# A two-layer graph network on one core: the turn from the edge sums to layer 1 in another order

## The reference, cut to what matters

```python
h = max(layernorm(x), 0)
agg = segment_sum(edge_attr_64, dst) / max(count, 1)        # per node, width 64
x = x + (relu(concat([agg, h]) @ W1 + b1) @ W2 + b2)         # layer 0, hidden width 512
h = max(layernorm(x), 0)
neigh = segment_sum(h[src], dst) / max(deg, 1)
x = x + (h @ w_self.T + b_self + neigh @ w_neigh.T)          # layer 1
```

## Time and profile before

| | us |
|---|---|
| median of 3 runs | 1263.76 (1263.55 to 1265.26) |
| the profiled execution | 1267.12 |
| its span in the profile | 1265.2 |
| PE busy | 1182.2 |
| DVE busy | 786.3 |
| ACT busy | 517.8 |
| POOL busy | 422.6 |

### The profile page before, as it was taken

The page is one execution under the profiler, slowest core; times in us unless marked ns, Lnnn a source line. Parts: engine busy times, 40 slices in busy tenths (PEclk is TensorE's granted clock), DMA queues, the critical chain, the costliest instruction groups (busy, mean ns, idle before and its releaser), DMA issues.

```text
span 1265.2 us, 31863 instructions
## 1 busy us (share of the span) xinstructions
PE 1182.2 (93%) x11708; PEld 928.3 (73%) x11708; DVE 786.3 (62%) x1710; ACT 517.8 (41%) x982; POOL 422.6 (33%) x384
## 2 busy tenths in 40 slices
PE   2879999999999899779999999999999999999997
PEld 1778888888888788647777767777776776777774
DVE  3537566566666455576666676666666676675762
ACT  3582133233233135344444444444444444444441
POOL 3001010010100166234634545435444453453451
PEclk9878999999999899879999999999999999999999
DMA  3895444444444411111212212112122121121221
GB/s 109 267 313 164 133 115 127 118 124 133 115 125 118 161 57 57 44 47 55 76 55 63 68 55 70 55 54 74 55 63 63 54 75 55 52 77 55 63 63 41
DMA packets 67053, 116.03 MB, mean 92 GB/s; under 512 B 10644, under 2 KB 30824, under 8 KB 66962
## 3 DMA queue, kind: packets, MB, share of 16 engines
q1 hardware_dynamic: 51922, 75.12, 19.5%
q0 software_dynamic: 15040, 39.80, 11.3%
HBM read 101.93 MB, written 12.95 MB: 91 GB/s over the span
## 4 chain that ended last, share of the span: by engine, by line
PE 80%; DVE 5%; DMA 5%; issue 3%; POOL 3%; DVEq 2%; ACT 2%; SPq 0%; ACTq 0%
PE bank L1093 33%; PE couples L888 14%; PE couples L1086 9%; PE bank L1112 7%; PE bank L923 6%; PE bank L913 4%; POOL kreg L570 3%; PE bank L911 3%; PE bank L1104 2%; DMA kreg<-in_edge_attr_dram 1%; DVE oreg L1518 1%; DMA hreg<-in_dst_dram 1%; DMA kreg<-in_src_dram,startu 1%; PE bank L1124 1%; PE couples L880 1%
## 5 line engine op out<-in xcount | busy, mean ns | idle before, releaser
L1093 PE MATMUL bank<-hreg,areg 128*128 128x512 f16 x2058 | 504.9, 382 | 0.0
L588 POOL DMA_INDIRECT wide<-h_table,aggn x280 | 324.6, 1159 | 400.3 <-PE couples L1086 230.4
L770 ACT ACTIVATE areg<-couples 128x784 bf16<-128x784 f32 x336 | 276.4, 823 | 376.7 <-PE couples L1086 375.0
L1093 PEld LDWEIGHTS bank<-hreg,areg 128*128 128x128 bf16 x2058 | 265.7, 144 | 104.6 <-issue 1.3
L888 PEld LDWEIGHTS couples<-oreg,kreg 128*64 128x64 f32 x3232 | 208.7, 145 | 44.4 <-issue 32.1
L888 PE MATMUL couples<-oreg,kreg 128*64 128x48 f32 x3232 | 220.4, 230 | 19.8 <-DMA kreg<-in_edge_attr_dram 11.2
L1518 DVE TENSOR_TENSOR oreg<-iota,kreg 128x1024 bf16<-128x1024 f16 x336 | 195.7, 624 | 51.5 <-PE couples L1086 49.9
L1518 DVE TENSOR_TENSOR hids<-iota,kreg 128x1024 bf16<-128x1024 f16 x336 | 196.3, 625 | 45.0 <-PE couples L1086 44.7
L889 PE MATMUL couples<-oreg,ones 128*64 128x48 bf16 x1616 | 202.0, 213 | 0.0
L889 PEld LDWEIGHTS couples<-oreg,ones 128*64 128x64 bf16 x1616 | 168.3, 109 | 0.0
L555 POOL TENSOR_TENSOR xr<-xr,b2bc 128x512 f32 x25 | 32.5, 1301 | 336.3 <-ACT h0buf L674 336.3
(11 more groups left out here) (165 smaller groups left out, 1048.2 us busy)
## 6 DMA issues: line engine op xcount, KB each, us to landing
kreg<-in_edge_attr_dram SPq DMA_DIRECT2D x202, 256.0 KB, 2.9
h_table<-hreg SPq DMA_DIRECT2D x25, 256.0 KB
xr<-in_x_dram SPq DMA_DIRECT2D x6, 1024.0 KB, 7.9
out_dram<-hbuf SPq DMA_DIRECT2D x42, 128.0 KB
wide<-h_table,aggn POOLq DMA_INDIRECT x280
wide<-in_L_gnn_W_dram SPq DMA_DIRECT2D x2, 512.0 KB, 6.7
out_dram<-h0buf SPq DMA_DIRECT2D x6, 128.0 KB
hreg<-in_dst_dram SPq DMA_DIRECT2D x1, 512.0 KB
```

Of the source, the lines that this page charges most:

```text
L588: pool.indirect_dma_start(near[:, k, :], None, table, bass.IndirectOffsetOnAxis(ap=nearsrc[:, n * GHALF + k:n * GHALF + k + 1], axis=0)).t ...
L770: act.activation(step.rearrange("p (a k) -> p a k", a=2), cpl[s % 2][:, :, 0:BC * KEYS], ACT.Copy).then_inc(s_adj, 1)
L1093: ins = pe.matmul(bank[4 + par], adj[:, par, :, h], htab[:, h, :], start=(h == 0), stop=(h == TN - 1))
```

## The change

On TensorE the 50 count transposes are split: 36 (the tiles of pairs 0 to 8, whose counts are final by then) are issued after the last `outer` of the last span, before the branch; 14 stay behind the wait for the finished `acc`. They go to bank 3 rather than bank 0. In `layer0` of pairs 9 to 11 `outer(i, 0)` stands ahead of the first `key_transposes`. `couples(0, 0)` and `couples(0, 1)` stand ahead of `outer(12, 0)`. On VectorE `low_part` stands ahead of `keys` in pairs 8 to 10; pair 11 has moved in among the first one-hots, and `low_part(12, 0)` behind the eighth. On ScalarE pair 11's two `h1` have moved behind `copy_places(2)` and `hidden(12, 0)`, in among the first copies of counts. TensorE has a wait for the table at step 5 of dense product 1, where ScalarE's wait for the same two semaphores is still ahead of its first copy for the next tile.

```diff
             layer0(BESIDE)                    # ScalarE
-            for n in range(3):
+            for n in range(2):
                 layer0(KEY0 + n, n)
+            hidden(U // 2 - 1, 0)
+            hidden(U // 2 - 1, 1, own=1)
+            copy_keys(2)
+            for q in range(2):
+                sd_of(U // 2 - 1, q)
+            copy_places(2)
             hidden(U // 2, 0)
...
             for s in range(ST):
-                if s == 2:
+                if s < 2:
+                    h1(U // 2 - 1, s)
+                if s == 4:
                     sd_of(U // 2, 0)
                     h1(U // 2, 0)
                 copy_counts(0, 0, s)
...
+                        if j == 16 and size < SPAN * SLOTS:   # TensorE, the last span
+                            complete_counts()
...
             pe.wait_ge(s_acc, 1)
-            for t in range(T):
-                ins = pe.transpose(bank[0][:, t:t + 1], acc[FE:FE + 1, t * P:(t + 1) * P], ident[FE:FE + 1, FE:FE + 1])
-            ins.then_inc(s_cntp, 1)
+            counts_by_node(4 * (BESIDE + 1), T).then_inc(s_cntp, 1)
...
+                outer(i, 0, 0)
+                outer(i, 0, 1)
                 if n is not None:
                     key_transposes(n, key16[n % 2], s_keytr)
-                for q in range(2):
-                    outer(i, q, 0)
-                    outer(i, q, 1)
+                outer(i, 1, 0)
+                outer(i, 1, 1)
...
+            hidden(U // 2, 0, 0, own=1)
+            hidden(U // 2, 0, 1, own=1)
             for s in range(ST):
                 couples(0, s)
                 if s == 1:
+                    outer(U // 2, 0, 0)
+                    outer(U // 2, 0, 1)
                     near_transposes()
...
+                        if first and s == 5:
+                            pe.wait_ge(s_tab[1], U // 2)
+                            pe.wait_ge(s_tab[0], U // 2 + 1)
...
+                low_part(i, 0)                 # VectorE, layer0
+                low_part(i, 1)
                 if n is not None:
                     keys(n)
-                low_part(i, 0)
-                low_part(i, 1)
...
+            last = U // 2
+            mean_by(last, 0)
             dve.wait_ge(s_loT, 1)
-            for s in range(ST):
+            dve.wait_ge(s_keys, NK)
+            one_hots(0, 0)
+            x1_stats(last - 1, 0)
+            x1_stats(last - 1, 1)
+            ln1(last - 1, 0)
+            ln1(last - 1, 1)
+            one_hots(0, 1)
+            near_in()
+            one_hots(0, 2)
+            low_part(last - 1, 0)
+            one_hots(0, 3)
+            x1_stats(last, 0)
+            ln1(last, 0)
+            one_hots(0, 4)
+            low_part(last - 1, 1)
+            near_out()
+            for s in range(5, ST):
                 one_hots(0, s)
-                if s == 1:
-                    near_in()
-                    x1_stats(U // 2, 0)
-                    ln1(U // 2, 0)
-                if s == 3:
-                    low_part(U // 2, 0)
-                    near_out()
+            low_part(last, 0)
```

More of the change, by code:

```diff
@@ L926, in outer, with counts_by_node, complete_counts @@
                     ins.then_inc(s_outp[q], 1)
+            def counts_by_node(t0, t1):
+                for t in range(t0, t1):
+                    ins = pe.transpose(bank[3][:, t:t + 1], acc[FE:FE + 1, t * P:(t + 1) * P], ident[FE:FE + 1, FE:FE + 1])
+                return ins
+            def complete_counts():
+                pe.wait_ge(s_h0T, U)
+                for q in range(2):
+                    pe.wait_ge(s_agg[q], BESIDE + 1)
+                counts_by_node(0, 4 * (BESIDE + 1))
             parts = {0: (hidden, 0, 0), 2: (hidden, 0, 1), 4: (hidden, 1, 0), 7: (hidden, 1, 1),
@@ L1054, in _ @@
                 layer0(KEY0 + n, n)
[L1055 to L1058, removed]
             def near_transposes():
@@ L1363, in mean_by, with layer0 @@
                                   bank[0][0:FE, q * NM:(q + 1) * NM], ALU.mult).then_inc(s_agg[q], 1)
-            def layer0(i, n=None, means=all_means, last=False):
+            def layer0(i, n=None, means=all_means):
                 means(i + 1, 0)
-                if not last:
-                    means(i + 1, 1)
+                means(i + 1, 1)
                 x1_stats(i, 0)
@@ L1477, in _ @@
             dve.wait_ge(s_cntp, 1)
-            dve.tensor_copy(cntN[:, :], bank[0][:, 0:T]).then_inc(s_cnt, 1)
+            dve.tensor_copy(cntN[:, :], bank[3][:, 0:T]).then_inc(s_cnt, 1)
             dve.wait_ge(s_cntT, 1)
@@ L1503, in _ @@
             dve.tensor_scalar(startu[:, :], bank[0][:, 0:DB], float(E - SL), None, ALU.min).then_inc(s_start, 1)
-            for n in range(4):
-                layer0(BESIDE + n, n if n < NK else None, means=mean_by, last=(n == 3))
+            for n in range(NK):
+                layer0(BESIDE + n, n, means=mean_by)
             def twice(n, k):
```

## The result

| | before | after |
|---|---|---|
| median | 1263.55 | 1274.26 |
| runs | 1259.02 to 1266.53 | 1266.68 to 1277.73 |
| profiled execution, span | 1267.12, 1265.2 | 1277.73, 1275.9 |

The ratio after to before is 1.0078, with an interval of [1.0049, 1.0106]: the change makes the kernel 0.8% slower. The forecast was 1252.4 us and faster. It was wrong in size and in sign.

What follows compares the result with a forecast made beforehand. TensorE bounds layer 1; the turn (first gather to the loop's first couples product) is bound by gathers, third `keys`, then pairs 11 and 12. Gain 0.2 + 5.1 + 4.3 + 2.7 - 0.9 = 11.4: 1263.76 to 1252.4 us, range 1250.4 to 1256.8.

Steps and rivals of the forecast that it cites:

- The change leaves its rhythm alone: Layer 1: TensorE is the bound there, busy 698.0 of 713.6 us, and the change does not alter its rhythm.
- the same 713.6 us from there to the end: Sign to look for: from the loop's first couples product to the end, layer 1 still takes 713.6 us.
- The branch costs at most the same 1.67 again: TensorE before the 14 late count transposes: branch costs at most 1.67 us, the last ends at 430.4, nothing on the path moves.
- The slower rival: Start of layer 1: TensorE's clock stays low longer, each step costs 1.5 us more, some 28 us could be lost; chance 3%.
- Count transposes: 0: Splitting the 50 count transposes before the first gather moves nothing on the path: 0, with 2.3 us of cover.
- Low parts ahead of keys: 0.2: VectorE, pairs 8 to 10: gathers still set the third `keys`, which ends 0.2 us earlier, at 511.2 (bounds 510.7 and 512.5).
- Half of `outer` ahead: 5.1, 3.5 of it the half and 1.5 the clock: TensorE, pair 11: half of `outer` fills the wait for the third `keys`; 4.3 us remain behind it instead of 9.4.
- given back at the clock: Rival: TensorE's clock falls despite the 1.9 us idle, or a hand-off costs a ScalarE turn; gain 7.5 to 9.5 us; chance 13%.
- ScalarE's order 4.3, clock in `outer(12)` 2.7, -0.9 between: 6.1: End of the turn: earlier ReLU of pair 12 4.3 us, full clock in its `outer` 2.7, -0.9 from there to the loop.
- The new wait, the stores: 0: Step 5 wait of dense product 1 costs 0; SyncE's earlier last store gives 0, or at most 1 us inside an unawaited burst.
- Sum of the turn: Gain of 11.4 us up to the loop's first couples product, which begins at 540.2 in place of 551.6.

Runs made afterwards that it cites:

- e2: Kernel after without the 36 count transposes in TensorE's branch that is not taken: ratio to before 0.9921, turn 104.6 us, layer 1 713.4.
- e4: Kernel before with only the count transposes split 36 and 14, no copy in the branch not taken: ratio 0.9995, turn 114.8 us.
- e3: Kernel after with all 50 count transposes back behind the wait for the sums, in bank 0: ratio to before 0.9892, turn 104.4 us.
- e10: e3 with the low parts behind `keys` as before: ratio to the kernel before 0.9917, turn 104.4 us.
- e9: Kernel before with only VectorE's low parts ahead of `keys` in pairs 8 to 10: ratio 1.0080, turn 124.5 us.
- e8: Kernel before with only the first half of `outer` ahead of the key transposes in pairs 9 to 11: ratio 0.9984, turn 111.4 us.
- e7: Kernel after with 74 more never-run transposes in the branch not taken, 110 in all: ratio to before 0.9914, turn 102.1 us.
- e12: Kernel before with only pairs 11 and 12 interleaved with the first couples steps on all engines: ratio 0.9941, turn 108.1 us.
- e1: Kernel before with 36 transposes added in TensorE's branch that is not taken: ratio 1.0102, layer 1 729.7 us.
- e6: Kernel before with 18 transposes added in the branch not taken: one run, 1285.55 us, layer 1 731.1.
- e11: Kernel before with 56 transposes added in the branch not taken: one run, 1279.66 us, layer 1 730.2.
- e13: Kernel before with 164 transposes added in the branch not taken: one run, 1280.37 us, layer 1 729.8.
- e16: Kernel before with 92 transposes added in the branch not taken: one run, 1296.37 us, layer 1 746.1.

## Why the prediction was wrong

*"The change leaves its rhythm alone", and "the same 713.6 us from there to the end".* This is the step that failed, by 18.9 us. In it layer 1 had one thing that could differ, the clock at its start. Code that is never run had no price, though the diff shows `complete_counts()` written out a second time and the page's queue 8 counts the instruction packets. *"The branch costs at most the same 1.67 again"* saw instruction loading once, at the start of the count transposes, and not at the branches of the longest loop. No rival and no part of the range held it. The slower rival had the right stage but the wrong mechanism: at the start of the loop the clock stood at 0.50 for 3.9 us, in the kernel after too, and was full again within 5 us in both. What the runs showed in its place: with the loop's code moved against the blocks by the 36 transposes that never run, TensorE waits 2.7 to 3.0 us for instructions at each of the four taken branches, 16.5 us with the clock behind three of them, and e2, which takes only those transposes out, has layer 1 at 713.4 again.

*Count transposes: 0.* The work, yes (e4: turn 114.8, whole kernel 0.9995). In the kernel after the last ended at 433.9 where 430.4 was forecast, since they came in pieces behind the branch, with waits for "issue" before each:

```profile
429.50 0.47 PE L940 MATMUL couples<-ident,areg 1*128 1x1 f32 x3 [2.49 <-issue]
432.61 1.33 PE L940 MATMUL couples<-ident,areg 1*128 1x1 f32 x11 [2.63 <-issue]
```

VectorE copied `cntN` at 433.97 where it had at 432.72, and the first gather began at 437.90 in place of 436.64. In e2, without the second copy of the code, the copy of `cntN` comes at 432.94 again. So 1.3 of the 1.4 us between the gain of the turn, 9.4, and the lead at the loop's start, 8.0, are probably again the place of code; that these pieces fall on block borders is argued, not shown.

*Low parts ahead of keys: 0.2.* e3 against e10: 104.4 and 104.4; a term of 0.2 is too small for one execution of each. Nothing blocked the gathers that can be seen: from the first to the last edge index they take 62.4 us in e3 and 64.1 in e10. The term's reason held only beside the swap of `outer`: counted from the first gather, the low parts of pair 10 were forecast to end at 65.2, and end at 64.9 in e3, but at 76.6 alone (e9).

*Half of `outer` ahead: 5.1, 3.5 of it the half and 1.5 the clock.* The half is right: 3.6 in e8. The clock is not: with 2.51 us idle in front TensorE fell to 0.68 for the next 5.4, and the half took 5.36 where 3.5 were forecast. The rival "given back at the clock" had this mechanism. It costs 1.5 of the sum (3.6 for 5.1). The step that failed here is the idle time in front, 1.9 in the forecast: 2.51 in the kernel after and 2.24 in e2, and the clock fell in both. In e7, which executes the same instructions, the third `keys` came earlier, and the forecast of this term held:

```profile
505.87 0.56 PE L1045 MATMUL couples<-ident,wide 128*128 128x128 f16 x7 [0.68 <-DVE wide L1384]
506.26 3.67 PE L931 MATMUL bank<-wide,hids 128*128 128x256 f32 x16
```

Counted from the first gather, these transposes begin at 73.7 us there, at 74.5 in e2 and at 75.5 in the kernel after; that execution has the shortest turn, 102.1. So whether this term comes hangs on differences of under 2 us between executions.

*ScalarE's order 4.3, clock in `outer(12)` 2.7, -0.9 between: 6.1.* Measured 6.9 (e12). The split doesn't follow from the prediction's own times: `outer` of pair 12 at 521.8 for 530.3 is 8.5 earlier, 5.3 of them already counted, so ScalarE's order is worth 3.2 and the part behind that product +0.2; their sum, 3.4, is the same. In e12, counted from the first gather, `outer` of pair 12 starts 3.2 earlier than before, takes 2.5 less, and 1.2 more are gained behind it. It ran its 16 matmuls in 3.69 us, 3.5 forecast; here in the kernel after:

```profile
525.77 3.69 PE L931 MATMUL bank<-wide,hids 128*128 128x256 f32 x16 [0.30 <-ACT hids L646]
```

*The new wait, the stores: 0.* The turn of e2 and e3 leaves nothing for them; neither was tried apart.

*Sum of the turn.* 11.4 forecast; 10.6 in e3, 10.4 in e2, 9.4 in the kernel after and 12.9 in e7. In e3, 1.5 less from the clock, 0.2 less from the low parts and 0.8 more from the interleave make the difference, though the last two are smaller than what turns differ by from one execution to the next. With the loop where it was, the change is worth 0.8 to 1.1% (e2, e3, e7), near the 0.9% forecast; the reordering was priced about right in total, with errors in its terms that partly cancel. The 8.0 us of lead at the start of layer 1, and as much again, were lost at four branches.

## What to carry to other kernels

Where a loop's code is large, count its instructions and ask how many blocks it touches from where it starts. An edit in front of it, also in a branch that is never taken, can cost more than everything that is reordered, as here; the sign in a profile is the count of instruction packets, and a wait for "issue" in front of the first instruction of each round. Test it by adding or removing unexecuted instructions, before a verdict on the edit itself. When an operation is moved ahead of a wait, look whether what it needs hangs by other engines on the work behind that wait.

## What the runs showed of the hardware

- A taken branch behind which TensorE had to wait for instructions cost 2.7 to 3.2 us of idling each time (kernel after, e1, e6, e11, e13), and in the kernel after 4.4 to 4.5 with the clock at half behind it (3.1 at the first, behind which it did not fall); two such waits in a row cost 2.75 + 2.33 in e16. The branch instruction itself took 3.30 to 3.59 us in the kernel after and 0.21 to 0.23 in the kernel before.
- TensorE ran a loop of 1726 instructions without a packet of queue 8 for over 400 us where it lies in 7 blocks of 16384 bytes, and had 9 packets in each round where it touches 8.
- Where the loop lies decides: slow with 18, 36, 56, 92 and 164 unexecuted transposes, quick with 0, 110, 128 and 238. This fits the period of 128 (256 instructions, 16384 bytes) that was predicted for the last runs; if the slow places form one connected stretch, these nine values by themselves put the period between about 110 and 146.
- How long TensorE idled did not alone decide whether its granted clock fell: it fell behind 2.24 us (e2, turn), 2.51 us (kernel after, turn) and 2.89 us (layer 1), and not behind 2.08 us, nor behind the 3.03 us of the first branch.
